# A fixed order of four interleaved attention layers, replaced by another one; row buffers cleared later

## The reference

```python
attn = softmax(einsum('bnd,bmd->bnm', q, k) * scale);  out = einsum('bnm,bmd->bnd', attn, v)     # layers 0, 1, 2
Kn, Qn = K/|K|, Q/|Q|;  out = gamma * (V.sum + Qn (Kn V)) / (N + Qn . Kn.sum)                     # layer 3
```

## Time and profile before

| | |
|---|---|
| median of 3 runs | 6742.29 us (6739.93 to 6744.71) |
| profiled execution, its own time | 6743.66 us |
| its span, first to last instruction | 6741.8 us |
| granted TensorE clock, mean over the span | 0.969 |
| TensorE busy | 6224.2 us of the span |
| VectorE, ScalarE, GpSimd busy | 4059.2, 4181.9, 3427.5 us |

### The profile page before, as it was taken

One profiled execution on the slowest core, in us unless ns is written; L12 is line 12 of the kernel. 1 busy time (PEld: TensorE's weight loads), 2 busy tenths in 40 slices (PEclk: granted clock), 3 DMA queues, 4 the chain that ended last, 5 costly groups with the idle time before them and its releaser, 6 DMA issues.

```text
span 6741.8 us, 80368 instructions
## 1 busy us (share of the span) xinstructions
PE 6224.2 (92%) x29648; PEld 2907.3 (43%) x29648; DVE 4059.2 (60%) x4659; ACT 4181.9 (62%) x5828; POOL 3427.5 (51%) x2737
## 2 busy tenths in 40 slices
PE   5799999999999999999999999999999999999986
PEld 2334444444444444444444444444444444444433
DVE  1566666666666666666666666666666666666541
ACT  2456666666666666666666666666666666666652
POOL 4335555555555545555555555554555554555433
PEclk7899999999999999999999999999999999999997
DMA  1001101101101101110110110110110110110100
GB/s 33 13 14 27 24 14 27 27 17 27 23 18 23 26 17 27 23 23 17 27 25 18 23 27 14 27 26 17 27 23 14 26 27 17 27 23 14 23 14 7
DMA packets 95783, 145.66 MB, mean 22 GB/s; under 512 B 60320, under 2 KB 62496, under 8 KB 95264
## 3 DMA queue, kind: packets, MB, share of 16 engines
q1 hardware_dynamic: 95392, 140.53, 9.5%
HBM read 18.07 MB, written 16.78 MB: 5 GB/s over the span
## 4 chain that ended last, share of the span: by engine, by line
PE 74%; DVE 13%; ACT 4%; POOL 4%; issue 4%; DMA 0%; SPq 0%; POOLq 0%; ACTq 0%; DVEq 0%
PE p_chain L1158 17%; PE p_max L1158 15%; PE p_sc L1158 14%; PE p_full L1158 10%; PE p_acc L1158 10%; PE p_head L1158 9%; DVE mx_half L1003 7%; ACT p L867 2%; POOL t_rn L726 1%; DVE f2mx L998 1%; ACT fp L836 1%; DVE f0mx L998 1%; POOL fsum L715 1%; POOL fp_lo L694 1%; DVE ka L1095 1%
## 5 line engine op out<-in xcount | busy, mean ns | idle before, releaser
L1003 DVE TENSOR_REDUCE mx_half<-p_max 128x2 f32<-128x1024 f32 x2048 | 2509.8, 1225 | 1764.4 <-PE p_max L1158 1758.9
L867 ACT ACTIVATE p<-p_head 128x1024 f32<-128x1024 f32 x2048 | 2099.6, 1025 | 1265.7 <-PE p_head L1158 1247.6
L694 POOL TENSOR_TENSOR fp_lo<-fp,fp_hi 128x512 fp32r<-128x512 f32 x1024 | 1310.9, 1280 | 1635.0 <-ACT fp L836 1629.5
L1158 PE MATMUL p_acc<-p,v 128*17 128x512 f32 x8192 | 1142.8, 615 | 0.9 <-ACT p L867 0.9
L1158 PE MATMUL p_max<-ks,qs 63*128 63x512 f32 x4096 | 988.2, 478 | 158.2 <-DVE mx_half L1003 148.8
L1158 PE MATMUL p_head<-qs,ks 64*128 64x512 f32 x4096 | 962.6, 465 | 43.9 <-ACT p L867 31.5
L715 POOL TENSOR_TENSOR fsum<-fsum,fp 128x512 f32<-128x512 f32 x768 | 991.5, 1291 | 0.0
L826 ACT ACTIVATE fp_hi<-p_sc 128x512 fp32r<-128x512 f32 x1024 | 610.6, 596 | 525.1 <-PE p_sc L1158 411.1
L1158 PEld LDWEIGHTS p_max<-ks,qs 63*128 63x128 f32 x4096 | 386.9, 185 | 919.2 <-DVE mx_half L1003 673.7
L1158 PEld LDWEIGHTS p_head<-qs,ks 64*128 64x128 f32 x4096 | 388.8, 187 | 762.0 <-ACT p L867 407.9
L836 ACT ACTIVATE fp<-p_sc 128x512 f32<-128x512 f32 x1024 | 610.3, 596 | 23.2 <-POOL fsum L711 22.9
(11 more groups left out here) (183 smaller groups left out, 8521.3 us busy)
## 6 DMA issues: line engine op xcount, KB each, us to landing
qs<-cq_hi SPq DMA_DIRECT2D x128, 256.0 KB, 4.9
ks<-ck_hi SPq DMA_DIRECT2D x128, 256.0 KB, 4.9
x_in<-x_dram SPq DMA_DIRECT2D x32, 512.0 KB, 3.4
qs<-cq_lo SPq DMA_DIRECT2D x64, 256.0 KB, 4.4
ks<-ck_lo SPq DMA_DIRECT2D x64, 256.0 KB, 5.2
out_dram<-x SPq DMA_DIRECT2D x32, 512.0 KB, 2.8
zrow<-rz SPq DMA_DIRECT2D x128, 16.0 KB
cw<-packed_dram SPq DMA_DIRECT2D x1, 1178.0 KB, 5.2
```

Of the source, the lines that this page charges most:

```text
L694: pool.tensor_tensor(fp_lo[u % 2][:, :], fp[u % 2][:, :], f32(fp_hi[u % 2][:, :]), ALU.subtract).then_inc(f.plo, 1)
L867: act.activation(p1[slot][:, 2 * pr:2 * pr + 2, :], P_HEAD[:, :].rearrange("p (e n) -> p e n", e=2), ACT.Exp, scale=float(DH) ** -0.5).the ...
L1003: dve.reduce_max(mx_half[:, pr, :, t, kh], P_MAX[:, :].rearrange("p (e n) -> p e n", e=2), AX.X)\
L1158: return pe.matmul(dst, lhsT, rhs, start=start, stop=stop)
```

## The change

Every number of the tables is replaced by another one, and two tables are new: `HEAD_SUM_MOVE` moves each of the 32 `s_pv` steps by itself, `FULL_SUM_MOVE` each of the 32 `f_pv` steps. With them the order of the steps on each engine differs: of 285 TensorE steps in a period 80 keep their place relative to the first, and none moves by more than 12 places. Which engine does a step, what a step does and what it waits for stay as they were. Apart from the order, GpSimd clears `qs` and `ks` last instead of first, after `s_ones` is complete; SyncE waits for them only before the first `stack`; and TensorE's first product into `P_ACC` reads a newly cleared half of `o1[0]` instead of `qs`.

```diff
-PLACE = dict(h0=4.3, hp0=3.14, h1=111.3, hp1=2.886, exp=-0.0, pv=4.0, out=4.1, ma=8.5, map=2.535,
-             mb=45.1, mbp=2.255, mc=63.8, mcp=2.412, md=100.7, mdp=2.666, me=125.2, mep=2.431,
-             read=1.2, turn1=100.9, turn0=201.0, stack0=44.8, stack1=149.9, fgather0=-0.4,
...
-             tp1=173.4, tt1=174.1, tp2=175.8, tt2=177.0, istat=20.3, iapply=20.7, frecip0=36.4,
...
-             gvar=82.3, gapply=84.3, frecip2=148.2, fout=160.0, tnorms=177.2, tkeys=183.4,
-             tmatrix=182.4, tkeep=183.4, tksum=186.7, tscale=189.1, store=198.2)
...
-MAX_MOVE = [-1.4, -2.8, -2.2, -2.2, -2.4, -3.2, -1.4, -1.7, 0.0, -0.3, 0.8, 1.4, 1.8, 2.7, 1.7,
-            0.2, 0.4, 1.4, 2.5, 1.5, 1.6, 1.3, -0.1, 1.9, 2.3, 4.4, 4.1, 3.9, 3.0, 2.2, 3.8, 2.3,
-            -2.6, -3.0, -4.9, -3.2, -4.8, -4.4, -3.3, -2.0, -0.9, -2.5, -2.2, -3.2, -3.5, -4.6,
-            1.6, 0.3, 0.7, 4.0, 3.3, 3.0, 2.8, 1.5, 2.1, 0.5, 0.4, -1.1, 0.3, -1.0, -2.8, -2.8,
-            -3.8, -5.2]
...
+PLACE = dict(h0=4.2, hp0=3.139, h1=111.45, hp1=2.884, exp=-0.09, pv=4.06, out=2.68, ma=7.77,
+             map=2.488, mb=44.45, mbp=1.702, mc=63.92, mcp=2.427, md=99.27, mdp=2.205, me=125.3,
+             mep=2.424, read=1.44, turn1=98.04, turn0=199.88, stack0=83.1, stack1=134.13,
+             fgather0=6.17, freturn0=25.01, fgather2=102.33, freturn2=104.14, both=5.28,
...
+             tt0=170.65, tp1=173.77, tt1=173.46, tp2=174.73, tt2=176.76, istat=17.69,
...
+             fout=159.58, tnorms=177.3, tkeys=180.14, tmatrix=184.17, tkeep=183.96, tksum=185.67,
...
+MAX_MOVE = [-1.71, -2.16, -2.69, -2.27, -2.25, -2.95, -4.39, -2.97, -2.89, 0.72, 0.38, 0.96, 1.6,
+            0.13, 0.19, 1.39, 2.63, 2.0, 0.27, -0.39, 0.91, -0.75, -2.52, 1.42, 1.07, 3.21, 3.55,
+            3.39, 1.91, 1.35, -0.14, 2.78, -4.21, -4.29, -6.04, -6.37, -7.85, -7.24, -7.86,
+            -4.64, -3.7, -3.26, -3.09, -4.06, -1.62, -2.03, 4.65, 5.44, 4.56, 3.81, 1.66, 2.97,
+            3.23, 2.19, 0.19, 0.04, -0.79, -0.99, -0.34, -1.14, -1.28, -2.01, -2.39, -3.45]
+HEAD_SUM_MOVE = [-1.83, -0.63, 7.63, 3.26, 5.72, 0.66, -0.2, 3.65, 0.84, 7.62, 1.47, -1.13, 2.89,
+                 5.26, 7.64, 0.26, -0.69, 1.13, 1.27, -0.35, -3.31, 5.76, 1.04, -2.19, -0.4,
+                 2.93, -1.88, 2.72, -1.8, 1.69, -0.24, -2.26]
...
+FULL_SUM_MOVE = {0: [6.03, 0.2, -2.76, 1.29, -1.51, 0.85, -2.84, -1.23, 1.78, 0.22, -1.29, 2.76,
+                     2.58, -3.42, -3.05, -0.69],
+                 2: [3.88, 6.47, 0.99, -0.71, 0.88, -0.89, -4.29, -0.6, 0.53, 1.47, -2.1, 0.23,
+                     -1.2, -0.4, 1.55, -3.56]}
...
@@ -478,7 +489,7 @@
                     v = 2 * T*r+u
                     t = (PLACE['h0'] + PLACE['hp0']*v if r < 2 else PLACE['h1'] + PLACE['hp1']*(v-4*T)) + HEAD_MOVE[v]
                     at(t, "s_scores", 0, r, u); at(t+PLACE['exp'], "s_exp", 0, r, u)
-                    if u % 2: at(t+PLACE['pv'], "s_pv", 0, r, u//2)
+                    if u % 2: at(t+PLACE['pv']+HEAD_SUM_MOVE[v//2], "s_pv", 0, r, u//2)
                 at(t+PLACE['out'], "s_out", 0, r)
             mb = M_BREAK
             for start, pace, lane in (('ma','map',[("m_max",0,(k,)) for k in range(32,mb)]),
@@ -499,7 +510,7 @@
                 for u in range(2 * T):
                     t = PLACE[f'f{layer}'] + PLACE[f'f{layer}p']*u + FULL_MOVE[layer][u]; pace = PLACE[f'f{layer}p']
                     at(t, "f_scores", k, u, layer); at(t+PLACE['fexp'], "f_exp", k, u, layer); at(t+PLACE['fplo'], "f_plo", k, u, layer)
-                    at(t+pace+PLACE['fpv'], "f_pv", k, u, layer); at(t+PLACE['fadd'], "f_add", k, u, layer)
+                    at(t+pace+PLACE['fpv']+FULL_SUM_MOVE[layer][u], "f_pv", k, u, layer); at(t+PLACE['fadd'], "f_add", k, u, layer)
                     if u % T == T-1: at(t+pace+PLACE['fmove'], "f_move", k, u//T, layer)
             for g, k in ((1,-1),(0,0)):
                 at(PLACE[f'gather{g}'], "o_gather", k, g); at(PLACE[f'recip{g}'], "o_recip", k, g); at(PLACE[f'return{g}'], "o_return", k, g)
@@ -565,6 +576,9 @@

                 sp.wait_ge(sem.p_hi, b.at(PER.p_hi, 4))
                 sp.wait_ge(sem.p_lo, b.at(PER.p_lo, 4))
+                if b.index == 0:
+
+                    sp.wait_ge(s_fill, 2)

                 after(sp, (sem.s_sc, b.shift(-1), PER.s_sc, 32 * (g + 1)))
                 pair, rows = slice(2 * g, 2 * g + 2), slice(HALF_C * g, HALF_C * (g + 1))
@@ -611,15 +625,12 @@
                 sp.wait_ge(sem.t_ev, b.at(PER.t_ev, 2))
                 sp.dma_start(one(out, b), x3[:, :]).then_inc(sem.stored, 16)

-            sp.wait_ge(s_fill, 2)
             play(sp, dict(load=load, stack=stack, m_row=m_row, o_gather=o_gather,
                           o_return=o_return, f_gather=f_gather, f_return=f_return, store=store))
             sp.wait_ge(sem.stored, 16 * images)

         @block.gpsimd
         def _(pool):
-            pool.memset(f32(qs[:, :, :]), 0.0).then_inc(s_fill, 1)
-            pool.memset(f32(ks[:, :, :]), 1.0).then_inc(s_fill, 1)
             pool.memset(ones[:, :], 1.0).then_inc(s_ones, 1)
             pool.memset(f32(ones_r[:, :]), 1.0).then_inc(s_ones, 1)
             pool.memset(minus_half[:, :], -0.5).then_inc(s_ones, 1)
@@ -627,11 +638,14 @@
             pool.memset(qa[:, :, D3:D3 + 1], 1.0).then_inc(s_ones, 1)
             pool.memset(ka[:, :, D3:D3 + 1], 1.0).then_inc(s_ones, 1)
             pool.memset(zpad[:, :], 0.0).then_inc(s_ones, 1)
+            pool.memset(o1[0][:, 0:HALF], 0.0).then_inc(s_ones, 1)
             for v in v1:
                 pool.memset(v[:, :, :, :], 0.0).then_inc(s_ones, 1)
-            pool.wait_ge(s_ones, 9)
+            pool.wait_ge(s_ones, 10)
             for v in v1:
                 pool.memset(v[:, :, :, DH:DH + 1], 1.0).then_inc(s_ones, 1)
+            pool.memset(f32(qs[:, :, :]), 0.0).then_inc(s_fill, 1)
+            pool.memset(f32(ks[:, :, :]), 1.0).then_inc(s_fill, 1)

             def g_var(b):
                 pool.wait_ge(sem.g_veps, b.at(PER.g_veps, 1))
@@ -891,7 +905,7 @@
                 act.activation(x3[:, half(h)], P_CHAIN[:, :], ACT.Copy).then_inc(sem.t_ev, 1)

             act.wait_ge(s_const, 32)
-            act.wait_ge(s_ones, 11)
+            act.wait_ge(s_ones, 12)

             act.wait_ge(s_fold, 6)
             act.activation(mat("wv0"), P_MAX[:, 0:C], ACT.Copy).then_inc(s_folded, 1)
@@ -1121,7 +1135,7 @@
                                   .broadcast_to([C, T, D3 + 1]), ALU.mult).then_inc(sem.t_qs, 1)

             dve.wait_ge(s_const, 32)
-            dve.wait_ge(s_ones, 11)
+            dve.wait_ge(s_ones, 12)

             dve.reduce_sum(lane_of[:, :], mat("ident").rearrange("p (j c) -> p j c", c=32), AX.X)\
                .then_inc(s_lanes, 1)
@@ -1413,7 +1427,7 @@
                 mm(P_CHAIN[:, :], ma[:, 0:C], qt3[:, 4 * h:4 * h + 4, :]).then_inc(sem.t_o, 1)

             pe.wait_ge(s_const, 32)
-            pe.wait_ge(s_ones, 11)
+            pe.wait_ge(s_ones, 12)
             mm(P_MAX[:, 0:C], mat("wv0"), mat("wp0")).then_inc(s_fold, 1)
             mm(P_MAX[:, C:C + 1], mat("wp0"), col("bv0")).then_inc(s_fold, 1)
             mm(P_MAX[:, C + 1:C + 2], mat("wp1"), col("bv1")).then_inc(s_fold, 1)
@@ -1424,8 +1438,7 @@
             mm(P_FULL[:, 0:1], turn, col("bq1"))
             mm(P_FULL[:, 1:2], turn, col("bk1")).then_inc(s_fold, 1)

-            pe.wait_ge(s_fill, 2)
-            mm(P_ACC[:, :], mat("ident"), f32(qs[:, 0, 0:HALF]))
+            mm(P_ACC[:, :], mat("ident"), o1[0][:, 0:HALF])
             pe.wait_ge(s_folded, FOLDS)
             play(pe, dict(g_average=g_average, p_average=p_average, f_qk=f_qk, f_value=f_value,
                           p_qk=p_qk, p_value=p_value, f_max=f_max, m_max=m_max, m_turn=m_turn,
```

More of the change, by code:

```diff
@@ L60 @@
-HEAD_MOVE = [3.1, 1.1, 0.3, 0.1, -0.7, -2.5, -3.2, -2.2, -2.0, -3.7, -4.1, -3.6, -4.2, -2.1,
[4 rows of a table removed]
-MAX_MOVE = [-1.4, -2.8, -2.2, -2.2, -2.4, -3.2, -1.4, -1.7, 0.0, -0.3, 0.8, 1.4, 1.8, 2.7, 1.7,
[4 rows of a table removed]
-FULL_MAX_MOVE = {0: [1.7, 0.7, 1.0, 0.3, 1.6, 2.2, 2.7, 1.3],
-                 2: [-5.5, -6.3, -5.3, -5.6, -1.3, -0.2, 3.1, 2.4]}
-FULL_MOVE = {0: [-0.4, 0.3, -1.9, -1.2, -3.0, -1.5, -2.0, -2.5, -1.1, 0.4, 0.5, 2.3, 1.3, 0.2,
-                 0.2, 1.9],
-             2: [-5.5, -0.8, -0.5, 5.2, 4.0, 2.5, 1.7, 0.3, 0.4, -2.5, -3.2, -3.5, -3.9, -1.5,
-                 -2.4, -1.2]}
+PLACE = dict(h0=4.2, hp0=3.139, h1=111.45, hp1=2.884, exp=-0.09, pv=4.06, out=2.68, ma=7.77,
+             map=2.488, mb=44.45, mbp=1.702, mc=63.92, mcp=2.427, md=99.27, mdp=2.205, me=125.3,
+             mep=2.424, read=1.44, turn1=98.04, turn0=199.88, stack0=83.1, stack1=134.13,
+             fgather0=6.17, freturn0=25.01, fgather2=102.33, freturn2=104.14, both=5.28,
+             t_turn=9.14, t_neg=7.01, t_row=-19.33, sh2_0=49.64, sh0_0=127.13, sh2_1=69.43,
+             sh0_1=166.78, f2=60.78, f2p=5.163, f0=146.68, f0p=4.85, fexp=0.49, fpv=2.36,
```

(23 more changed lines are left out.)

27 lines of the change are left out of this document (7 added, 20 removed), and 9 rows, old and new, of the table HEAD_MOVE.

## The result

The changed kernel takes **6468.48 us** (median of 4 runs, 6465.19 to 6474.8) against 6742.3 for the kernel before beside it; the ratio is 0.9595, with a 95% interval of 0.9578 to 0.9612. That is 274 us less. The forecast was 6635 with a range of 6560 to 6712, and the rival of the largest gain stood at 6575: the sign was right, the size much too small.

A forecast was written before the change was run, and what follows sets the result against it. TensorE's waits in the steady state, 9.4 us per image, were what a new order could win. Terms of -2.7, -0.4, -0.7 and +0.3 gave -3.5 per image, times 30 images, plus 2 for the start: 6635 us, range 6560 to 6712.

The forecast's parts named there:

- `P_HEAD` + `P_SC`: TensorE's waits at these two buffers: counted 1.59 + 0.89 before, 1.87 + 0.78 after, taken as 0 change.
- `t_matrix`: TensorE's wait for GpSimd's power function and VectorE's scaling ahead of this step: all of it goes, -0.7 us per image.
- `P_MAX` at face value, -2.7 us: TensorE refilling `P_MAX` before VectorE has read it: counted short trips fall from 6.95 to 4.27 us per image.
- granted clock of 0.99: TensorE's clock between 3000 and 4000 us, read beside 95% busy time; no term in the sum.
- `P_CHAIN`, -0.4: Round trips of `f_qk` and `f_value` through this buffer: counted -0.6 us per image, taken as -0.4.
- the shift's way, +0.3: `m_turn` 0 to `s_scores(0, 0)`, through VectorE and a DMA: cover falls from 3.31 to 2.85, between 0 and +0.5 us per image.
- the distance is 199.87: Steady state: one image leaves every 199.87 us, read from one pair of starts of a layer 3 instruction.
- 9 us unexplained, as a bound: Image time beyond paces of 181.5 and waits of 9.4 us; its shrinking helps bound the gain at -5.5 per image.
- Start: Constants before the two fills: start up to 3.9 us earlier, half taken, -2 us once, bounds -3.9 and 0.
- The waits didn't move on: Rival: us saved at `P_MAX` are met by a full `P_HEAD` or `P_SC`; 6705 us, down to no change; chance 0.15.
- More than counted: Rival: all waits of 9.4 us shrink, or the lost 9 us too; -5.5 per image, 6575 us; chance 0.15.
- The late stack: Rival: SyncE's first `stack` waits behind `o_gather` 0 beyond a 2.2 us margin; slower, 6840 at 9 us late; chance 0.08.

The follow-up runs named there:

- e1: Changed kernel with the old order tables and the two new tables at zero, leaving only the later fills and their waits: 6739.8 us, 1.0002 of before.
- f2: Kernel before with `t_matrix` and its copy `t_keep` placed three TensorE steps later: 6712.5 us, 0.9965 of before.
- e4: Kernel before with four one-column VectorE instructions of the norms written with one input from memory: 6655.4 us, 0.9876 of before.
- k2: Kernel before with the product of `s_scores(1,2)` issued four times instead of once, ahead of a 1.7-us TensorE wait: 6697.5 us, 0.9929 of before.
- f1: Kernel before with one number changed, MAX_MOVE[54] from 2.1 to 0.2, putting an `f_scores` between `m_max` 54 and 55: 6679.9 us, 0.9915 of before.
- e10: Changed kernel with GpSimd alone kept in the old order: 6668.6 us, 0.9898 of before.
- e7: New order on TensorE and VectorE only; ScalarE, GpSimd and SyncE keep the old one: 7620.4 us, 1.1307 of before.
- e13: Changed kernel with SyncE alone kept in the old order, first `stack` ahead of `m_row` 1 and `o_gather` 0: 6468.6 us, 0.9602 of before.
- g2: Changed kernel with layer 1's first `p_qk` one TensorE step later: 6483.8 us, 0.9627 of before.
- e14: Changed kernel with the four one-column VectorE norm instructions written with one input from memory: 6472.4 us, 0.9603 of before.

## Why the prediction was right or wrong

**Right.** Steady state, not start or ends: e1 is 1.0002. TensorE's waits as the thing that an order can win, `P_MAX` as the largest of them, `P_HEAD` + `P_SC` nearly unchanged (0.68 to 0.83, forecast under 1.5), `t_matrix` (the wait gone, and f2 alone gives its size), `stack` (one wait of 0.5 us). Filling was costed at nothing, +/- 8: the first image's `ka` starts at 601.9 instead of 596.9, 5 us later.

**Step "`P_MAX` at face value, -2.7 us": the term was mis-sized.** It measured -5.3 (6.45 to 1.18). The count met the old total, and I took that as leave to trust it on the new order. But it had VectorE's work between two reads "as far as the time before doesn't hold it", with the durations of the trace of before, and these belong to the old order: `p_mv`, `p_ac` and `g_mv` of 0.92 to 1.17 us are 0.22 us long wherever no GpSimd instruction is in the middle. With 0.22 the count gives 5.41 for the old order (e4 measured 5.06) and 2.71 for the new one instead of 4.27. So -1.6 of the missing 2.6 is this duration. That it was the holds that made the old waits longer is shown by e4 and by the rows; its share in the new order is my count and no run. The last 1.0 is the count: it stood 0.5 too high on the old order and stands 1.5 too high on the new one, where the short trips that it names (2.71) show only 1.18 of wait.

**Step "granted clock of 0.99": read as full, and left out of the sum.** In finer slices it is 2.5 us an image, of which the distances show 1.6 (200.77 against 199.20 without a dip). It also hung on where TensorE stands idle: k2 fills one wait and wins 48 us with more work. Between before and after it is 1.2 us an image by the undipped distances, 1.7 by the granted clock. The earlier trace rows held both the 0.99 and the 1.73-us wait on which much of it hangs. The Trainium skill, page "TensorE: Matmul & The Clock Gate", section "A second HAM failure mode: psum-queue depth-cycling", says of a bf16 kernel that cycles through its result banks that frequent short idles between groups of matmuls make the clock swing between its two levels. This case agrees in kind: less idle time went with fewer dips in f1 (31 to 10) and k2 (31 to 8). I had not weighed it.

**Steps "`P_CHAIN`, -0.4" and "the shift's way, +0.3": neither came.** Without the wait behind `ka`, which went as forecast (-0.7), the recorded waits at `P_CHAIN` are 1.32 us an image before and 1.41 after. The two ScalarE waits of the earlier trace rows, for which the term stood, fell by 1.0 (from 1.32 to 0.30), but three others came that the count hadn't named: for `hx` (0.67), `p_mv` (0.23) and `x` (0.21). For the shift's way no wait is recorded at all.

**Step "the distance is 199.87".** One distance is no mean where the distances come in three sizes; over 22 images it was 200.77. This put the unexplained rest at 9 us and hid that it varied with the image.

**Step "9 us unexplained, as a bound".** I kept it for the bound and a rival and gave the sum nothing from it. It shrank by 2.6: by 0.8 at steps that have a recorded wait, whose wait costs more than its idle time (11.68 us lost at 9.52 recorded before, 5.08 at 3.73 after), and by 1.8 at steps without one, mostly ahead of `m_max` (3.5 to 2.7) and `s_scores` (1.7 to 1.3). The split by step rests on my paces, I only accounted for this part, and no run isolates it.

**Start: half of 3.9 us taken, 0.4 measured.** The weight copies did stand behind a fill, queued after two small copies that it held. The rule of the Trainium skill, page "SBUF — State Buffer", section "Who interferes with whom", had said that copies in the two-port mode would, and this trace agrees: 3.52 us for two copies of 128 by 8 beside a fill of 3.51. Whether they run in that mode no row shows. By the rule the sum would have been 2 us smaller, and nearly right in this term.

**The rivals.** The waits didn't move on, but for the one to `hx`: e10 and e7 show what it looks like when they do, and there it is `P_FULL` and `P_SC`, not `P_HEAD`. "More than counted" had the right sign, and its reason was part of the truth: lost time that the count doesn't name. Even so it stopped at 5.5 of 9.6 us: it lacked the held instructions and the clock. The late stack is refuted by e13 and by the row above.

**The sum with what was measured**, per image: recorded waits -5.8 (`P_MAX` -5.3, `ka` -0.7, the rest +0.2), time beside them -2.6, dips -1.2: -9.6. Forecast were -3.8 of waits, +0.3 for the shift, and nothing for the other two. No version tried beats the changed kernel: g2 is slower, and e13 and e14 are the same within a measurement.

## What to carry to other kernels

Before durations of a trace are used for another order, ask of each that is long for its size whether another engine's instruction ends at the same moment; if so, its length belongs to the order and not to the instruction. Where TensorE's clock is anything below 1.00 in a stretch, read it in slices of a microsecond beside the waits: a wait can cost its idle time once and as much again in speed (f1: 0.8 us of waits, 2.0 us of distance), so two waits of the same length need not be worth the same. Take the distance of one period as a mean over many, and look at how it is spread.
